# The turned copies of layer 1's weights are made on GpSimd instead of ScalarE

## What is computed

```
x = x + conv9x9(group_norm(x), gaussian_kernels(L0_conv_weight)) + bias   # zero padding 4
x = x + conv5x5(group_norm(x), L1_conv_weight)                            # reflect padding 2
```

## Time and profile before

| | |
|---|---|
| median of 3 runs | 252.07 us |
| the profiled execution, its own time | 252.27 us |
| its span, first to last instruction | 250.5 us |
| TensorE busy | 227.5 us (91%) |
| VectorE busy | 215.5 us (86%) |
| ScalarE busy | 155.1 us (62%) |
| GpSimd busy | 6.6 us (3%) |
| mean granted clock of TensorE | 0.986 of full |

### The profile page before, as it was taken

One profiled execution on the slowest core, in us unless ns is written; L12 is line 12 of the kernel. 1 busy time (PEld: TensorE's weight loads), 2 busy tenths in 40 slices (PEclk: granted clock), 3 DMA queues, 4 the chain that ended last, 5 costly groups with the idle time before them and its releaser, 6 DMA issues.

```text
span 250.5 us, 4075 instructions
## 1 busy us (share of the span) xinstructions
PE 227.5 (91%) x1400; PEld 140.9 (56%) x1400; DVE 215.5 (86%) x468; ACT 155.1 (62%) x326; POOL 6.6 (3%) x14
## 2 busy tenths in 40 slices
PE   0075999998999999997999999999999999999994
PEld 0074466665566566554666666555666665655552
DVE  4979998899999989999989979999995278978942
ACT  5986788587679755996937693357466002658310
POOL 1030000040000000000000000000000000000000
PEclk9999599999999999999999999999999999999999
DMA  6970132311005200015302000045020000621123
GB/s 179 415 288 0 42 88 52 73 45 42 0 3 138 67 3 0 1 29 157 115 1 97 0 0 4 0 131 171 11 85 3 0 0 18 179 103 47 51 94 96
DMA packets 9189, 17.71 MB, mean 71 GB/s; under 512 B 3408, under 2 KB 6096, under 8 KB 9168
## 3 DMA queue, kind: packets, MB, share of 16 engines
q1 hardware_dynamic: 8352, 17.16, 21.2%
q10 hardware_dynamic: 816, 0.29, 0.4%
HBM read 5.51 MB, written 4.72 MB: 41 GB/s over the span
## 4 chain that ended last, share of the span: by engine, by line
PE 51%; DVE 33%; ACT 7%; issue 5%; DMA 2%; DVEq 0%; SPq 0%; ACTq 0%
PE banks L1273 27%; PE banks L1290 24%; DVE X L694 7%; ACT junk L972 5%; DVE lo L661 3%; DVE whl L511 2%; DMA X<-in_x 2%; DVE work L506 1%; ACT hi L1013 1%; DVE wl L536 1%; DVE partU L603 1%; DVE g2t L516 1%; DVE ps L684 1%; DVE s L622 1%; DVE partU L610 1%
## 5 line engine op out<-in xcount | busy, mean ns | idle before, releaser
L1273 PE MATMUL banks<-hi,whl 128*128 128x360 f16 (+4 forms) x576 | 100.7, 325 | 5.7 <-ACT hi L1013 5.7
L1273 PEld LDWEIGHTS banks<-hi,whl 128*128 128x128 f16 x576 | 56.7, 100 | 41.1 <-issue 8.6
L1273 PE MATMUL banks<-lo,whl 128*128 128x376 f16 (+4 forms) x288 | 52.4, 323 | 0.0
L972 ACT ACTIVATE junk<-X 128x576 bf16<-128x576 f32 x60 | 40.9, 681 | 2.7 <-DVE X L694 0.5
L1273 PEld LDWEIGHTS banks<-lo,whl 128*128 128x128 f16 x288 | 28.4, 99 | 17.6 <-issue 0.8
L1290 PE MATMUL banks<-lo,wh 128*128 128x384 f16 x160 | 31.6, 328 | 0.0
L1290 PE MATMUL banks<-hi,wl 128*128 128x384 f16 x160 | 31.6, 328 | 0.0
L1290 PE MATMUL banks<-hi,wh 128*128 128x384 f16 x160 | 31.6, 328 | 0.0
L1013 ACT CAST hi<-s 128x384 f16<-128x384 f32 x32 | 15.4, 509 | 22.3 <-DVE s L622 9.5
L1013 ACT CAST hi<-work 128x416 f16<-128x416 f32 x32 | 16.6, 538 | 18.0 <-PE banks L1290 11.5
L1003 ACT ACTIVATE work<-work,gof,gsc 128x26 f32<-128x26 f32 (+1 forms) x48 | 23.3, 576 | 3.6 <-DVE gof L587 3.6
(11 more groups left out here) (124 smaller groups left out, 229.6 us busy)
## 6 DMA issues: line engine op xcount, KB each, us to landing
X<-in_x SPq DMA_DIRECT2D x8, 576.0 KB, 9.5
out<-X SPq DMA_DIRECT2D x7, 576.0 KB, 3.0
work<-X SPq DMA_DIRECT2D x8, 432.0 KB, 3.9
whl<-work SPq DMA_DIRECT2D x32, 64.0 KB, 2.0
work<-X SPq DMA_DIRECT2D x8, 144.0 KB, 3.6
stage<-in_w SPq DMA_DIRECT2D x1, 640.0 KB, 7.5
work<-X SPq DMA_DIRECT2D x32, 12.0 KB, 2.4
out<-X SPq DMA_DIRECT2D x1, 384.0 KB, 2.6
```

What stands on the lines that cost most here:

```text
L972: nc.scalar.activation(waste, image(n, m), function, accum_out=sums[c][:, col:col + 1]).then_inc(sums_done[c], 1)
L1273: ins = nc.tensor.matmul(dst[:, :, o0:o1], w[1][:, i, t * P:(t + 1) * P], src[:, :, o0 + dx:o1 + dx], start=(first and part == 0 and t == ...
```

## The change

`turn_kernel` moves from ScalarE's program to GpSimd's, with the same waits and the same semaphore. Its 16 calls leave ScalarE's list. On GpSimd they run in FIRST_ORDER, wh before wl, behind `normalise_last(0)`; `normalise_last(1)` stands behind the copies of stream 5, so the copies of stream 6 stand behind it. The DMAs, their queue and their order are as before.

```
@@ ScalarE
-            def turn_kernel(i, part):
-                at = FIRST_ORDER.index(i)
-                act.wait_ge(wh1_done if part is wh else wl1_done, at + 1)
...
-                nc.scalar.copy(dst, src).then_inc(turning, 1)
...
             high_half(1, 0, 0)
-            turn_kernel(1, wh)
-            turn_kernel(1, wl)
             high_half(1, 0, 1)
...
@@ GpSimd
             normalise_last(0)
-            normalise_last(1)
+
+            def turn_kernel(i, part):
+
+                at = FIRST_ORDER.index(i)
+                pool.wait_ge(wh1_done if part is wh else wl1_done, at + 1)
+                if at >= TURNS:
+                    pool.wait_ge(turned[MIRROR[FIRST_ORDER[at - TURNS]]], 16 * RB)
+                src = part[1][:, i, 0:PAD1 * P].rearrange("p (b o) -> p b o", o=C)[:, ::-1, :]
+                dst = turn_at[:, at % TURNS, 0 if part is wh else 1, :].rearrange("p (b o) -> p b o", o=C)
+                nc.gpsimd.tensor_copy(dst, src).then_inc(turning, 1)
+
+            for i in FIRST_ORDER:
+                turn_kernel(i, wh)
+                turn_kernel(i, wl)
+                if i == 5:
+                    normalise_last(1)
```

More of the change, by code:

```diff
@@ L1087, in _ @@
             high_kernel(2)
-            turn_kernel(2, wh)
-            turn_kernel(2, wl)
             high_half(1, 0, 2)
             high_kernel(0)
-            turn_kernel(0, wh)
-            turn_kernel(0, wl)
             channel_sums(1, 1, range(2, 3))
@@ L1096, in _ @@
             high_kernel(7)
-            turn_kernel(7, wh)
-            turn_kernel(7, wl)
             act.wait_ge(bias_loaded, 16)
@@ L1101, in _ @@
             high_half(1, 0, 4)
-            turn_kernel(3, wh)
             high_kernel(4)
-            turn_kernel(3, wl)
             channel_sums(1, 1, range(3, 4))
@@ L1107, in _ @@
             high_half(1, 0, 5)
-            turn_kernel(4, wh)
-            turn_kernel(4, wl)
             high_kernel(5)
             high_half(1, 0, 6)
-            turn_kernel(5, wh)
             high_kernel(6)
-            turn_kernel(5, wl)
             high_half(1, 0, 7)
             standard_deviation(1, 1)
-            turn_kernel(6, wh)
             normalise1(1, range(1))
-            turn_kernel(6, wl)
             normalise1(1, range(1, QI - 1))
```

## The result

The changed kernel takes 255.72 us (median of 4 runs, 255.40 to 256.09) against 252.07 before: ratio 1.0146, 95% interval 1.0134 to 1.0158, **3.65 us slower**. The profiled execution took 255.40 us, its span is 253.6 (3.1 more than before). The sign and both mechanisms of the forecast are in the trace; the size, +8.5 us, was more than double what came.

What follows compares the result with a forecast made beforehand. The prediction took VectorE to bound the kernel before and TensorE's late last stream after: 7.6 (lateness) + 2.9 (clock) - 1.95 (in hand) = +8.5 us, 260.6 us against 252.07, range 254.0 to 265.0.

Steps and rivals of the forecast that it cites:

- both mechanisms of the forecast: GpSimd's copies lengthen VectorE's instructions, and the last stream's copies come late behind `normalise_last(1)`, stopping TensorE.
- What bounds the kernel: VectorE runs without a gap from 44.5 to 118 us and sets the end; TensorE trails with 1.95 us to spare.
- Relief: ScalarE's lost copies end VectorE's 1.83 us wait at 44.49: 1.1 us directly, 0.7 us through VectorE's own delay.
- Cost of a read on VectorE: Each GpSimd copy of 512 elements costs VectorE 0.42 us, by elements; all 16 less 1.83 us give +4.9 us.
- Duration of a copy on GpSimd: Beside a dense VectorE a copy takes 1.8 us, ends 0.6 and 2.7 us, carried over from `tensor_scalar`.
- The late last stream: Stream 6's copies behind `normalise_last(1)` land at 68.5; TensorE waits 5.4 us and quad 1 starts 7.6 us later.
- The clock: After TensorE's stop the clock falls to half for 5.9 us of matmuls: +2.9 us, between 0 and 2.9.
- What TensorE had in hand: Waits of 0.21 and 1.74 us between 63 and 119 us, 1.95 us, absorb that much TensorE delay.
- The dear rival: GpSimd holds VectorE for its whole instruction: 16 x 1.05 - 1.83 = +15 us, 267 us; chance 0.06.
- side figure of 264: Time in us given if VectorE is held for half of the +15 us loss.
- 10.5 us late at quad 1: Delay of TensorE at quad 1: 7.6 us from the late stream plus 2.9 us from the clock.

Runs made afterwards that it cites:

- run 1: Kernel before without ScalarE's 16 turned copies and nothing in their place, DMAs reading the weights unreversed (output differs): 250.81 us, ratio 0.9946.
- run 2: Kernel before, ScalarE's copies kept, with GpSimd making the same 16 copies in addition into a spare tile nobody reads: 256.14 us, ratio 1.0156.
- run 7: Changed kernel with all sixteen copies still on GpSimd but `normalise_last(1)` behind them all, so the last stream is not late: 255.22 us, ratio 1.0122.
- run 9: Kernel before, all copies on ScalarE, with stream 3's two turned copies moved behind the high half of stream 4: 251.27 us, ratio 0.9964.
- run 10: Kernel before, all copies on ScalarE, with stream 3's turned copies and the sums over X moved behind stream 4's high half: 250.15 us, ratio 0.9921.
- runs 6: Changed kernel with stream 6's two copies back on ScalarE at their old places, the other fourteen on GpSimd: 254.73 us, ratio 1.0103.
- run 4: Kernel before plus 16 additional GpSimd copies into an unread tile, each 256 float32 in plain order instead of 512 reversed float16: 253.71 us, ratio 1.0060.
- runs 7 and 8: The second: changed kernel with 17 unread matmuls filling TensorE's stop ahead of the last turned part: 255.10 us, ratio 1.0118. For the first see run 7.
- run 5: Kernel before with only stream 6's two copies moved to GpSimd, behind `normalise_last(1)`; ScalarE keeps fourteen: 253.18 us, ratio 1.0042.

## Why the prediction was right in kind and wrong in size

- *What bounds the kernel*: right. Runs 1, 2, 7, 9 and 10 change VectorE's list or its wait and move the end by about as much, and ahead of the matmul that was at 119.36 TensorE still waits 1.73 to 1.74 us for that list in runs 6, 7 and 10.
- *Relief*: right. 1.1 us of the 1.83 us wait by itself (run 1), 1.5 us in the changed kernel, where VectorE's own delay covered a part of the rest. I had said all 1.83.
- *Cost of a read on VectorE*: the price was right, 0.41 us against 0.42, and by elements (run 4). The count was not: I charged all 16 copies in full, 6.7 us; 13 paid, some in part, 4.6 us. What I missed is that a copy beside an instruction with a PSUM input, or in a wait, is free (three of them), and that one which overlaps only in part costs less. At the statistics of quad 1 this makes the delay 2.6 us and not 4.05: the offsets are written at 55.26 against 53.14, in an execution whose beginning was 0.45 us earlier (GpSimd's first normalisation at 16.18 against 16.63).
- *Duration of a copy on GpSimd*: **this was the step that failed**. For lack of a row I took 1.8 us from the `tensor_scalar` and named 0.6 to 2.7 us as ends; it was 0.87 us. Two copies stand on the path of the last stream and took 1.81 us together where 3.6 were in the sum, so 1.8 us too much, the largest single miss; with it right the sum would still have been +6.7 us, and the count above and the clock below make the most of the rest. The row lay near in position but not in kind: a `tensor_scalar` of 336 elements with two operations took 1.69 to 1.84 us beside a dense VectorE, a copy of 512 took 0.88 to 1.14. Which property of the `tensor_scalar` makes it slow, no run tests. The Trainium skill, "GPSIMD Engine Reference", section "4.1 Engine selection" (one input, roughly line rate), fits better: 512 elements in 0.61 us at best.
- *The late last stream*: the mechanism was right to each link: normalisation 3.5 us, issue and landing 3.9 us (60.88 to 64.79), and a DMA as releaser. TensorE's stop was 2.75 us and not 5.4. But this path sets the end by only about 0.6 us: VectorE's path alone gives +3.0 to 3.1.
- *The clock*: it fell, as forecast, but the half-speed stretch was 3.4 us and cost 1.7 us, not 2.9.
- *What TensorE had in hand*: 2.36 us and not 1.95. I counted the waits shown as idle ahead of two matmuls; the distance from 79.85 to 119.36 shrank by 2.36.
- *The dear rival* was ruled out as priced: no VectorE instruction lost more than 0.41 us to one copy. Its side figure of 264 does not follow from its sum: half of +15 us gives 259.6. Nothing else rests on it.

The sum again: 10.5 us late at quad 1 was forecast. Less 1.8 (copies), 1.5 (VectorE), 1.2 (clock) and 0.45 (earlier beginning) leaves 5.55, where 5.48 was measured; less 2.36 in hand is 3.12, the loss of the span. So nearly all of the miss is in four sizes (copies, VectorE, clock, time in hand), none in the path. A sum along one chain adds every generous choice: the first three were inside the bounds that I had given, the fourth had none, and all four were off the same way.

How the 3.65 us part: about 3.0 to 3.1 are VectorE's list (runs 7 and 8), 0.5 to 0.6 the late stream. The two paths lie so close that taking either away shows little; they do not add.

## What to carry to other kernels

Work moved to GpSimd is not free for VectorE: each element that it reads while VectorE runs two-input instructions on SBUF took 0.8 ns from VectorE, so it pays only if VectorE is not the bound, or beside instructions that read PSUM. Before an engine is relieved, look which single wait its load causes; here 9.8 us of work on ScalarE was worth one wait of 1.83 us, and putting the step that is waited for ahead of its neighbours took it all, without moving any work. Where an engine's list gets a long wait, ask what stands behind it: two copies queued behind `normalise_last(1)` stopped TensorE for 2.75 us.

## What the runs showed of the hardware

- A GpSimd read delays a two-input VectorE instruction by the read's elements (0.20 us for 256, 0.26 to 0.32 for 336, 0.41 for 512), whatever their width, and not by the GpSimd instruction's own 0.4 to 1.8 us. GpSimd memsets of 0.52 us cost nothing. That the loser waits for the other's whole instruction, the rule of the page "SBUF — State Buffer" of the Trainium skill that I had weighed, is not what these runs show for VectorE: it lost 0.41 us to copies of 0.61 us and more. In the other direction the times fit: copies that began inside a two-input VectorE instruction took 0.09 to 0.53 us longer, about the rest of that instruction.
- A stop of TensorE of 2.6 to 2.9 us was followed by 3.4 us at half clock in two kernels (the changed one and run 5); in run 2, with a stop of 2.86 us, the stretch was twice as long, 1.96 + 2 + 2 + 0.88 = 6.8 us by the granted clock of these windows. Why it was, no run here settles; the kernel before has such a long stretch at its start too, behind its stop of 3.03 us. The stop of 1.79 us at 51.58 in the changed kernel was followed by none (granted clock 1.00 from 52 to 54).

```profile
52.00:54.00 2.00, 1.11 (x4) 0.51 0.24 57
54.00:56.00 2.00, 2.00 (x8) 0.50 0.00 0
56.00:58.00 2.00, 2.00 (x8) 0.50 0.45 107
58.00:60.00 2.00, 2.00 (x12) 0.78 0.19 46
```
